# Sixteen neighbouring partitions instead of every sixth one: where a tuned attention kernel stacks its split operands

## The reference

```python
ct_q = _lin(x, w_down_q, b_down_q)
q = (_lin(ct_q, w_up_q, b_up_q) + _rope(_lin(ct_q, wq_r, bq_r), cos, sin)).reshape(bs, sl, nh, hd)
ct_kv = _lin(x, w_down_kv, b_down_kv)
k = (_lin(ct_kv, w_up_k, b_up_k) + _rope(_lin(ct_kv, wk_r, bk_r), cos, sin)).reshape(bs, sl, nh, hd)
v = _lin(ct_kv, w_up_v, b_up_v).reshape(bs, sl, nh, hd)
scores = jnp.einsum('bqhd,bkhd->bhqk', q, k) / np.sqrt(hd)
probs = jax.nn.softmax(scores, axis=-1)
a = jnp.einsum('bhqk,bkhd->bqhd', probs, v).reshape(bs, sl, nh * hd)
...
x = x + _layernorm(attention(_layernorm(x)))
x = x + _layernorm(experts(_layernorm(x)))
```

## Time and profile before

| what | value |
|---|---|
| median of 3 runs | 429.7 us (428.06 to 430.42) |
| the profiled execution | 428.06 us |
| its span, first to last instruction | 426.2 us |
| PE busy | 396.7 us, 93% |
| DVE busy | 274.8 us, 64% |
| ACT busy | 207.7 us, 49% |
| mean share of the 16 DMA engines, queue of SP | 30.4% |
| bytes moved | 47.29 MB |

### The profile page before, as it was taken

The page is one execution under the profiler, slowest core; times in us unless marked ns, Lnnn a source line. Parts: engine busy times, 40 slices in busy tenths (PEclk is TensorE's granted clock), DMA queues, the critical chain, the costliest instruction groups (busy, mean ns, idle before and its releaser), DMA issues.

```text
span 426.2 us, 9422 instructions
## 1 busy us (share of the span) xinstructions
PE 396.7 (93%) x3383; PEld 298.6 (70%) x3383; DVE 274.8 (64%) x629; ACT 207.7 (49%) x383; POOL 129.6 (30%) x184
## 2 busy tenths in 40 slices
PE   7999789999999999797989999999999999999990
PEld 7675457676767766374759999999994444689970
DVE  5574577987879776776675693222226898728865
ACT  1744848576766757556551213344447676211100
POOL 1424414435162524303402002222212120037772
PEclk9999999999999999899999999999999999999996
DMA  8735226374734645350146640111111110123332
GB/s 264 212 108 143 60 70 197 91 206 103 214 95 124 188 116 191 95 182 7 47 154 231 232 151 27 37 39 50 50 51 51 51 40 27 51 75 111 115 99 86
DMA packets 50756, 47.29 MB, mean 111 GB/s; under 512 B 5334, under 2 KB 45526, under 8 KB 50710
## 3 DMA queue, kind: packets, MB, share of 16 engines
q1 hardware_dynamic: 44779, 38.31, 30.4%
q0 software_dynamic: 1632, 4.46, 3.6%
q10 hardware_dynamic: 4299, 3.92, 2.7%
HBM read 25.19 MB, written 8.65 MB: 79 GB/s over the span
## 4 chain that ended last, share of the span: by engine, by line
PE 75%; DVE 11%; issue 4%; POOL 3%; ACT 3%; DMA 2%; ACTq 0%; DVEq 0%; POOLq 0%
PE bank L1388 37%; PE bank L1707 7%; PE bank L1392 6%; PE bank L1556 5%; PE bank L1576 5%; PE bank L1517 5%; PE bank L1732 3%; DVE nmax L1057 2%; PE bank L1455 2%; PE bank L1503 1%; PE bank L1445 1%; DVE wall L1087 1%; DVE stacks L1358 1%; DVE stats_at L991 1%; POOL rstd_at L641 1%
## 5 line engine op out<-in xcount | busy, mean ns | idle before, releaser
L1057 DVE TENSOR_REDUCE nmax<-bank 128x2 f32<-128x512 f32 x112 | 74.3, 686 | 25.5 <-PE bank L1517 24.8
L1388 PEld LDWEIGHTS bank<-stacks,wall 128*128 128x128 f32 x512 | 59.8, 192 | 2.5 <-issue 1.9
L1388 PE MATMUL bank<-stacks,wall 128*128 128x128 f32 x512 | 61.2, 276 | 0.4 <-ACT stacks L909 0.4
L1263 DVE TENSOR_TENSOR stacks<-stacks,bank 128x512 f32<-128x512 f32 x34 | 23.4, 687 | 50.7 <-PE bank L1388 48.2
L873 ACT ACTIVATE pv<-bank 128x512 f32<-128x512 f32 x64 | 38.3, 606 | 34.2 <-PE bank L1576 33.3
L873 ACT ACTIVATE wall<-bank 128x512 f32<-128x512 f32 x64 | 38.5, 606 | 27.3 <-PE bank L1576 26.3
L909 ACT ACTIVATE stacks<-bank 128x512 f32<-128x512 f32 x34 | 20.3, 597 | 64.3 <-PE bank L1388 54.3
L1576 PE MATMUL bank<-stacks 99*128 99x256 bf16 x256 | 49.3, 275 | 2.2 <-ACT wall L873 2.1
L1388 PE MATMUL bank<-wall,stacks 128*128 128x256 f32 (+1 forms) x208 | 49.3, 381 | 0.0
L1517 PE MATMUL bank<-stacks 96*128 96x256 bf16 x224 | 42.8, 275 | 6.4 <-DVE nmax L1057 6.3
L706 POOL DMA_INDIRECT stacks<-x_sc,row_i x18 | 19.9, 1107 | 89.5 <-PE bank L1392 70.5
(11 more groups left out here) (207 smaller groups left out, 796.7 us busy)
## 6 DMA issues: line engine op xcount, KB each, us to landing
stacks<-low_sb SPq DMA_DIRECT2D x144, 64.0 KB, 2.0
wall<-gate_up SPq DMA_DIRECT2D x8, 1024.0 KB, 5.4
wall<-down SPq DMA_DIRECT2D x8, 512.0 KB, 6.7
y_exp<-stacks ACTq DMA_DIRECT2D x18, 128.0 KB, 1.7
x_tok<-wall SPq DMA_DIRECT2D x8, 256.0 KB, 2.5
stacks<-x_tok SPq DMA_DIRECT2D x16, 128.0 KB, 2.5
out<-stacks SPq DMA_DIRECT2D x8, 256.0 KB, 2.1
stacks<-low_sb SPq DMA_DIRECT2D x12, 128.0 KB, 2.4
```

The costliest lines, as they stand in the source:

```text
L1057: dve.tensor_reduce(nmax[:, half, qt, 2 * pair:2 * pair + 2], two(sm_bank[u % 2]), AX.X, ALU.max, negate=True).then_inc(sm["sm_max"], 1)
L1263: dve.tensor_tensor(to, sg, fu[:, :], ALU.mult).then_inc(sm["h_sb"], 1)
L1388: last = pe.matmul(out_ap, lhsT, rhs, start=(n == 0), stop=(n == len(pairs) - 1))
```

## The change

The destination rows of a slot r are changed, in both functions that stack. Before, slot r took rows r, r + 6, r + 12, ..., r + 90. Now it takes rows 16r to 16r + 15. The contraction sums over all 96 rows, and q's side and k's side are permuted in the same way, so each product stands in another row and the sum has the same terms. Number, size, source, order and waits of the DMAs stay, and every engine's list of instructions is the same length in the same order.

```diff
@@ whole
                                 sp.dma_start(
-                                    stacks[r:ROWS:NSLOT, b, side, :, :].rearrange("d h c -> d (h c)"),
+                                    stacks[HD * r:HD * r + HD, b, side, :, :].rearrange("d h c -> d (h c)"),
                                     parts_of(key, b)[:, part, :, :],
                                 ).then_inc(sm[f"stacked{b}"], 16)
@@ stack
                                     sp.dma_start(
-                                        half_of(stacks[r:ROWS:NSLOT, b % 2, side, :, :], m),
+                                        half_of(stacks[HD * r:HD * r + HD, b % 2, side, :, :], m),
                                         parts[key][:, part, m, :],
                                     ).then_inc(sm[f"stacked{m}"], 16)
```

## The result

The changed kernel takes 431.83 us (median of 8 runs, 431.09 to 433.57) against 428.8 for the one before on the same chip (8 runs, 427.51 to 430.42). The ratio is 1.0077, with a 95% interval of 1.0052 to 1.0101: 3.0 us slower. The forecast was 0.95 us slower, in a range up to 434.9. On the scale of the first runs (429.7) the measured step would give 432.7. So the sign came out and the size is three times the forecast's. Which parts of the forecast's mechanism held is told at the end.

What follows compares the result with a forecast made beforehand. PE, busy 93% of the span, was taken to bound the kernel. Terms 0.25 (stack, batch 4) + 0.3 (maxima, head 8) + 0.4 (four other waits) = 0.95 us, so 429.7 becomes 430.6; range 428.6 to 434.9.

Steps and rivals of the forecast that it cites:

- Mechanism: All 168 stack transfers: 16 neighbouring destination rows make transfers get in each other's way, so they land later.
- 128 KB, value taken 0.99 us: Stack transfers of batches 0 and 1: each taken at 0.99 us, halfway between bounds, against one issued each 0.65.
- Batch 0, cost 0, "with little left": Before the first head: last stack landing 4.1 us later, at 31.1, against 32.53; stack and maxima cost 0.
- The rival of the pile-up: Transfers nearly take turns, 1.25 us for 128 KB and 0.78 for 64 KB: 5.1 us slower, 434.8; chance 0.21.
- Batch 1, 1.1 us left, 0.3 for the maxima: Stack lands at 45.3, read at 46.45, cost 0; maxima for head 8 of batch 0 cost 0.3 us.
- 64 KB, engines held 0.60 us: Batches 2 to 7: 0.60 us a transfer, under the turn of 0.65, no backlog, each landing 0.34 us later.
- The one late place at 104.7, 0.25 us for the stack itself: Batch 4, half 0: stack landing has margin 0.0 to 0.2 us before its read at 104.74; cost about 0.25.
- 0.4 us put on four boundaries: Four of the five waits for the maxima: 0.1 us each for engines shared with the stack, of 0 to 1.4.
- The clock: Faster rival: small shifts fill the gap from 170.0 us and 1.7 us of half-clock time returns; 427.5, chance 0.04.
- Pile-up in the slots: Part of the slower rival: 64 KB blocks fall 1.6 us behind, cost 2.3 us, slots longer than 23.5; chance 0.21.

Runs made afterwards that it cites:

- e5: Against the kernel before: all 168 stack transfers write every second partition instead of every sixth; 428.43 us, ratio 0.9988.
- e8: The changed kernel run once more, nothing altered; 432.92 us, ratio 1.009 to the kernel before.
- e1: Against the kernel before: only the 24 transfers of 128 KB (batches 0 and 1) write neighbouring rows; 431.72 us, ratio 1.0039.
- e2: Against the kernel before: only the 144 transfers of 64 KB (batches 2 to 7) write neighbouring rows; 430.73 us, ratio 1.0019.
- e10: Against the changed kernel: the maxima for head 0 of batch 0 are issued by ACT instead of SP; 431.56 us in one run.
- e9: Against the kernel before, old layout kept: only SP's transfer of the maxima for head 0 of batch 0 is held back; 431.49 us, ratio 1.0061.

## Why the prediction was right in sign and short in size

**Mechanism.** Neighbouring destination rows slow the transfers down, with nothing else changed: right. e5 changes the rows in the same two places and loses nothing, so it is which partitions a transfer's 16 rows take that does it.

**128 KB, value taken 0.99 us.** Measured 1.10 by the landings. A small miss, but the backlog grows with the difference to 0.65, and already the first transfer landed 1.0 us later, which the sum didn't have. So the last transfer of batch 0 fell behind by 5.8 us (32.8 against 27.0), not 4.1.

**Batch 0, cost 0, "with little left".** This is the term that failed. The margin of 5.5 us was used up by the stack alone: it landed at 32.8, after the old start of head 0 at 32.53, where the sum had it at 31.1. The maxima, queued behind it, had been waved through, and landed at 33.3. Head 0 lost 0.95 us in this execution (0.59 in e8's, for the stack). The rival of the pile-up had its threshold at 1.1 us a transfer and "some 0.5 more for the maxima", and the measured 1.10 lies on it. In batch 0 that rival was the better description.

**Batch 1, 1.1 us left, 0.3 for the maxima.** Landing 46.1 (forecast 45.3), no wait of L1517, 0.15 us at head 8, and nothing there in the executions of e1 and e8. Right in the main.

**64 KB, engines held 0.60 us.** Wrong: the engines were held no longer than before (28.8 ns a packet). The landing still came 0.4 to 0.5 us later (0.34 forecast). So the time that packets hold an engine was the wrong measure for a landing. That the writes go on after the packet's record ends would explain it, and no run shows it directly. e2 has the price, 0.6 ± 0.4 us.

**The one late place at 104.7, 0.25 us for the stack itself.** The place was right. In the result's execution the maxima were late there, by 0.36 us, and not the stack, which landed at 104.8 + 2.4 = 107.2 before L1517 read it at 107.73. In the executions of e2, e8 and e10, with the same 64 KB layout, L1517 waited for the stack itself, and in e2 and e8 that cost 0.31 and 0.38 us: the forecast's mechanism, near its size. Of the 0.4 us put on four boundaries little else showed: up to 0.04 at the others in the result's execution, and 0.17 at the one before in e8's.

**The clock.** It stood among the rivals as a gain, and not in the sum as a loss. About half of the 3.0 us went with it. That is the largest single term missing: the direct parts were 0.95 forecast and about 1.5 measured, the clock 0 forecast and about 1.5 measured.

**Pile-up in the slots.** Did not happen; the slots of batches 3 to 6 kept their length to 0.04 us.

**Sign and luck.** The sign was forecast from the right effect, but 0.95 of the 1.46 us direct in the result's execution came from batch 0, to which the forecast gave nothing, and its own total of 0.95 us is the same number by chance.

## What to carry to other kernels

Where small DMAs write few partitions, count how many of the rows of one transfer fall into one aligned group of four partitions (with the group 32 off): two were free here, three and four were not, and a stride of two was as good as one of six. When a stream of transfers gets slower, check the margin of its last transfer and that of the last small one queued behind it: here either came last, by the execution. And where PE runs close to full, put a price on added idle time through the clock too: in e9 a wait of 1.5 us in the first batch went with 2.8 us in the median.

## What the runs showed of the hardware that was not expected

A packet's recorded time need not show when its data has landed. The 512-byte packets took 28.8 ns in the neighbouring layout and 28.7 in the spread one, while landings moved from 2.0 to 2.5 us. Only the 1 KB packets were stretched (53.4 to 118 ns). And spreading rows wider made transfers slower: 2.5 us to landing with every second partition, 3.4 with every third.
